# A four-layer graph network on one core: buffers, order and engines of the normalisation in the first and last node phase

## What is computed

```python
# layer 0: skip = per-irrep linear of x, weighted by the node's attribute; an angle from the summed messages
#          gives cos and sin, and  out = cos(angle) * skip + sin(angle) * summed
x = layernorm(x + layer_0(x, ...))          # over the 160 features, eps 1e-5
# layer 3:
fs   = silu(out_s[:, :64])
gate = sigmoid(out_s[:, 64:96])
gv   = gate[:, :, None] * out_v             # 32 vectors of 3
x = layernorm(x + concat(fs, gv))
```

## Time and profile before

| | |
|---|---|
| median of 3 runs | 6049.73 us (6048.89 to 6055.41) |
| the profiled execution | 6039.83 us, of which its span is 6038.1 us |
| TensorE busy (share of the span) | 5207.7 us (86%) |
| VectorE busy | 4336.6 us (72%) |
| ScalarE busy | 3091.9 us (51%) |
| GpSimd busy | 3854.7 us (64%) |
| DMA | 139 GB/s over the span |

### The profile page before, as it was taken

The page is one execution under the profiler, slowest core; times in us unless marked ns, Lnnn a source line. Parts: engine busy times, 40 slices in busy tenths (PEclk is TensorE's granted clock), DMA queues, the critical chain, the costliest instruction groups (busy, mean ns, idle before and its releaser), DMA issues. The chain is left out here.

```text
span 6038.1 us, 126869 instructions
## 1 busy us (share of the span) xinstructions
PE 5207.7 (86%) x29532; PEld 4038.8 (67%) x29580; DVE 4336.6 (72%) x15122; ACT 3091.9 (51%) x6650; POOL 3854.7 (64%) x4249
## 2 busy tenths in 40 slices
PE   8898977659999799699978888679999989997776
PEld 6565656655666699577756566568888867776766
DVE  3577759874444488688867777568888877775988
ACT  5333327763444366444444443257777744443766
POOL 8687866656888688776614554556666668885222
PEclk9899989998999899899987777789999999998999
DMA  8577766655666676354533333223333335554665
GB/s 321 137 127 119 123 119 224 221 173 112 133 132 126 174 230 227 119 161 157 162 115 83 88 88 89 70 93 108 114 108 108 114 80 86 87 88 90 228 225 184
DMA packets 547954, 837.00 MB, mean 139 GB/s; under 512 B 200220, under 2 KB 298612, under 8 KB 544436
## 3 DMA queue, kind: packets, MB, share of 16 engines
q1 hardware_dynamic: 397235, 666.91, 35.1%
q0 software_dynamic: 150528, 167.91, 16.5%
HBM read 464.00 MB, written 369.33 MB: 138 GB/s over the span
## 5 line engine op out<-in xcount | busy, mean ns | idle before, releaser
L1162 POOL DMA_INDIRECT xg<-x,gidx x588 | 611.0, 1039 | 243.1 <-issue 169.9
L339 POOL DMA_INDIRECT agg<-summed,cidx x392 | 632.2, 1613 | 201.9 <-issue 113.1
L422 DVE TENSOR_TENSOR pr<-pf,ws 128x512 f32<-128x512 f32 x196 | 135.5, 691 | 463.3 <-PE pf L509 356.4
L1337 ACT ACTIVATE ob<-po 128x416 f32<-128x416 f32 (+1 forms) x392 | 197.7, 504 | 353.9 <-PE po L1414 176.9
L1173 POOL DMA_INDIRECT agg<-summed,cidx x196 | 316.4, 1615 | 77.7 <-issue 57.6
L1822 POOL DMA_INDIRECT old_a<-agg,cidx_a x196 | 188.8, 963 | 262.9 <-DMA agg<-new_a,cidx_a 109.4
L1828 POOL DMA_INDIRECT agg<-new_a,cidx_a x196 | 194.8, 994 | 238.5 <-DVE new_a L1924 183.8
L538 PEld LDWEIGHTS pc<-ob,same 128*128 128x128 f32 x1960 | 276.1, 192 | 81.1 <-issue 81.1
L2112 PE MATMUL pk_n<-wsb,xta_n 128*128 128x192 f32 x784 | 222.7, 368 | 112.0 <-ACT xtb_n L2127 112.0
L2205 POOL TENSOR_TENSOR rs_n<-ve_n,wsb 128x4 f32<-128x4 f32 x98 | 98.8, 1008 | 336.8 <-DVE nm_n L2193 336.8
L1400 PE MATMUL ph<-esT,wsb 128*128 128x512 f32 x588 | 303.0, 597 | 2.4 <-DMA trow<-in_src_r 2.4
(11 more groups left out here) (366 smaller groups left out, 17869.3 us busy)
## 6 DMA issues: line engine op xcount, KB each, us to landing
ar_n<-agg SPq DMA_DIRECT2D x194, 322.0 KB
agg<-zero SPq DMA_DIRECT2D x50, 768.0 KB
ar_n<-agg SPq DMA_DIRECT2D x97, 384.0 KB
agg<-zero SPq DMA_DIRECT2D x50, 704.0 KB
ar_n<-agg SPq DMA_DIRECT2D x97, 352.0 KB
agg<-zero_h SPq DMA_DIRECT2D x25, 1288.0 KB, 5.4
agg<-zero SPq DMA_DIRECT2D x50, 644.0 KB
x<-xn_n SPq DMA_DIRECT2D x97, 324.0 KB, 2.5
```

What stands on the lines that cost most here:

```text
L339: pool.indirect_dma_start(agg, bass.IndirectOffsetOnAxis(ap=cidx[r][:, t:t + 1], axis=0), summed[u][:, t, :], None, compute_op=ALU.add).th ...
L1162: pool.indirect_dma_start(xg[s][r][:, t, 0:XR], None, x, bass.IndirectOffsetOnAxis(ap=gidx[s][r][:, t:t + 1], axis=0)).then_inc(gathered[r ...
L1337: a.activation(ob[u][:, t, :], po[:, t % 2, 0:TW], ACT.Copy).then_inc(ob_ok, 1)
```

## The change

In both phases `y`, `mv`, `rs` and `nr` get four buffers (index r % 4), and the waits that guard them reach back to chunk c - 4 instead of c - 2. VectorE's variance step is gone: GpSimd makes `ve` and `nm` at the start of its deviation, behind a new wait for the join. ScalarE normalises one turn later (lag 5 for 4, and 4 for 3). In node phase 0 GpSimd's factors run one turn later (lag 2 for 1), and the sines wait for ScalarE's own cosine of the turn before. In node phase 3 ScalarE makes `ga` = `gt` + 1 in an instruction of its own, from a constant column `one`, and VectorE's gate is one product over all four t. Node phase 1 starts with eight `fence` steps on VectorE.

```diff
@@ node_phase_01
-        y = each(2, sb, "y", [P, T, D])
+        y = each(4, sb, "y", [P, T, D])
-        mv = sb("mv", [P, T, 2])
+        mv = each(4, sb, "mv", [P, T, 2])
-        rs = each(2, sb, "rs", [P, T])
-        nr = each(2, sb, "nr", [P, T])
+        rs = each(4, sb, "rs", [P, T])
+        nr = each(4, sb, "nr", [P, T])
@@ scalar
                 a.wait_ge(cf_ok, due(NCF * (c - 1)))
+                a.wait_ge(sc_ok, 2 * c)
...
-            node_pipeline(a, ((0, copy_turned), (4, normalise)) + (((1, sines),) if l == 0 else ()))
+            node_pipeline(a, ((0, copy_turned), (5, normalise)) + (((1, sines),) if l == 0 else ()))
@@ vector
-                v.wait_ge(xn_ok, due(T * (c - 1)))
+                v.wait_ge(xn_ok, due(T * (c - 3)))
...
             def join(c, r, k, parts):
-                v.wait_ge(ve_ok, 2 * c)
+                v.wait_ge(rs_ok, due(2 * (c - 3)))
                 v.wait_ge(st_ok, 8 * c + 4)
                 fence(v)
                 for t in range(T):
-                    v.bn_aggr(mv[:, t, :], st[:, t, :]).then_inc(st_ok, 1)
-
-            def variance(c, r, k, parts):
-                u = r % 2
-                v.wait_ge(st_ok, 8 * c + 8)
-                v.wait_ge(rs_ok, due(2 * (c - 1)))
-                v.tensor_scalar(ve[u][:], mv[:, :, 1], EPS, None, ALU.add).then_inc(ve_ok, 1)
-                v.tensor_scalar(nm[u][:], mv[:, :, 0], -1.0, None, ALU.mult).then_inc(ve_ok, 1)
-
-            node_pipeline(v, ((3, skips), (3, sums), (3, moments), (3, join), (3, variance)))
+                    v.bn_aggr(mv[r % 4][:, t, :], st[:, t, :]).then_inc(st_ok, 1)
+
+            node_pipeline(v, ((3, skips), (3, sums), (3, moments), (3, join)))
@@ gpsimd
             def deviation(c, r, k, parts):
                 u = r % 2
-                pool.wait_ge(xn_ok, due(T * (c - 1)))
-                fence(pool)
+                pool.wait_ge(xn_ok, due(T * (c - 3)))
+                fence(pool)
+                pool.wait_ge(st_ok, 8 * c + 8)
+                fence(pool)
+                pool.tensor_scalar(ve[u][:], mv[r % 4][:, :, 1], EPS, None, ALU.add).then_inc(ve_ok, 1)
+                pool.tensor_scalar(nm[u][:], mv[r % 4][:, :, 0], -1.0, None, ALU.mult).then_inc(ve_ok, 1)
                 pool.wait_ge(ve_ok, 2 * c + 2)
                 fence(pool)
-                pool.tensor_tensor(rs[u][:], ve[u][:], wt("mhalf"), ALU.pow).then_inc(rs_ok, 1)
+                pool.tensor_tensor(rs[r % 4][:], ve[u][:], wt("mhalf"), ALU.pow).then_inc(rs_ok, 1)
...
-            node_pipeline(pool, ((1, factors), (3, deviation), (1, attribute)) + (((0, angles),) if l == 0 else ()))
+            node_pipeline(pool, ((2, factors), (3, deviation), (1, attribute)) + (((0, angles),) if l == 0 else ()))
@@ node_phase_1, vector
+            for _ in range(LEAD):
+                fence(v)
@@ node_phase_3 (buffers, join and deviation as above)
+        ga = each(2, sb, "ga", [P, T, V1])
+        one = sb("one", [P, 1])
@@ scalar
                 a.activation(sg[u][:, :, 0:S0], ss[u][:, :, 0:S0], ACT.Silu).then_inc(act_ok, 1)
+                a.wait_ge(act_ok, 3 * c + 1)
+                a.activation(ga[u][:], gt[u][:], ACT.Identity, bias=one[:, 0:1], scale=1.0).then_inc(act_ok, 1)
...
-            node_pipeline(a, ((0, copy_turned), (3, normalise), (1, gates)))
+            a.wait_ge(folded, 3)
+            node_pipeline(a, ((0, copy_turned), (4, normalise), (1, gates)))
@@ vector
+            v.memset(one[:], 1.0).then_inc(folded, 1)
...
-                for t in range(T):
-                    last = v.scalar_tensor_tensor(sg[u][:, t, S0:D].rearrange("p (u c) -> p u c", c=3), gt[u][:, t, :].unsqueeze(2).to_broadcast([P, V1, 3]), 1.0,
-                                                  sv[u][:, t, :].rearrange("p (u c) -> p u c", c=3), ALU.add, ALU.mult)
-                last.then_inc(sg_ok, 1)
+                v.tensor_tensor(sg[u][:, :, S0:D].rearrange("p t (u c) -> p t u c", c=3), sv[u][:].rearrange("p t (u c) -> p t u c", c=3),
+                                ga[u][:].unsqueeze(3).to_broadcast([P, T, V1, 3]), ALU.mult).then_inc(sg_ok, 1)
```

More of the change, by code:

```diff
@@ L44 @@
 VW = 168
+LEAD = 8
 EPS = 1e-5
@@ L675, in normalise @@
                 for t in range(T):
-                    a.activation(xn[r][:, t, 0:D], y[u][:, t, :], ACT.Identity, bias=nr[u][:, t:t + 1], scale=rs[u][:, t:t + 1]).then_inc(xn_ok, 1)
+                    a.activation(xn[r][:, t, 0:D], y[r % 4][:, t, :], ACT.Identity, bias=nr[r % 4][:, t:t + 1], scale=rs[r % 4][:, t:t + 1]).then_inc(xn_ok, 1)
             if l == 0:
                 a.wait_ge(folded, 4)
-            node_pipeline(a, ((0, copy_turned), (4, normalise)) + (((1, sines),) if l == 0 else ()))
+            node_pipeline(a, ((0, copy_turned), (5, normalise)) + (((1, sines),) if l == 0 else ()))
         @block.vector
@@ L2114, in skip @@
                 last.then_inc(k_ps, 1)
-            pe.wait_ge(folded, 2)
+            pe.wait_ge(folded, 3)
             node_pipeline(pe, ((0, turn_rows), (1, skip)))
@@ L2141, in normalise @@
                 for t in range(T):
-                    a.activation(xn[r][:, t, :], y[u][:, t, :], ACT.Identity, bias=nr[u][:, t:t + 1], scale=rs[u][:, t:t + 1]).then_inc(xn_ok, 1)
-            node_pipeline(a, ((0, copy_turned), (3, normalise), (1, gates)))
+                    a.activation(xn[r][:, t, :], y[r % 4][:, t, :], ACT.Identity, bias=nr[r % 4][:, t:t + 1], scale=rs[r % 4][:, t:t + 1]).then_inc(xn_ok, 1)
+            a.wait_ge(folded, 3)
+            node_pipeline(a, ((0, copy_turned), (4, normalise), (1, gates)))
         @block.vector
         def _(v):
+            v.memset(one[:], 1.0).then_inc(folded, 1)
             v.tensor_scalar(wt("na_3")[:, 96:192], wt("na_3")[:, 96:192], 0.5, None, ALU.mult).then_inc(folded, 1)
```

36 lines of the change are left out of this document (18 added, 18 removed).

## The result

The changed kernel takes 6013.6 us in the median of five runs (6001.69 to 6021.03), the kernel before 6048.89 in the five runs that stand for it now (6041.1 to 6055.41): 0.9945 of it, with a 95% interval of 0.9933 to 0.9956. That is faster by 33 us by the ratio and by 35 us by the medians, inside the stated range, but 22 us above the forecast of 5992. The profiled execution's span is 6011.6 us, against 6038.1.

What follows compares the result with a forecast made beforehand. Phase 0 was taken as bound by a GpSimd-ScalarE ring, phase 3 by VectorE. Savings of 45.6 us (phase 3) and 12.6 (phase 0) sum to 58 off the 6049.7 median, giving 5992; range 5966 to 6022.

Steps and rivals of the forecast that it cites:

- a ring of GpSimd and ScalarE: Node phase 0 before: GpSimd's at, rs, nr, then ScalarE's normalising and sines, back to at; 4.39 us a turn.
- VectorE's own turn: Node phase 3 before: VectorE itself sets the pace, 4.60 us a turn with no idle time named in the rows.
- the second rival: Phase 0 gains nothing or loses (0 to +16 us), GpSimd's path being too long; phase 3 as forecast; 6004 to 6020; chance 0.24.
- (a) the gate: Node phase 3, VectorE: four gate instructions become one 128x384 product, gate to total 0.89 to 0.68 us, saving 0.21 a turn.
- The fourth rival: Phase 3's one product runs at the dear row's 840 ns: -17 us there, phase 0 -30, so 6020; chance 0.11.
- (b) the join: Node phase 3: constant and negation leave VectorE, join to next layer 0.67 to 0.41 us, saving 0.26 (0.17 to 0.34).
- ScalarE's and the DMA's room: Node phase 3: ScalarE's work grows to 3.5 us, under 4.14; DMA rises from 224 to 249 GB/s, with room for loads.
- ScalarE's wait for nr: Node phase 3: 140.8 us before; its being gone was named as a sign that the forecast is right.
- 0.17 + 0.43 = 0.6 us: Node phase 0, GpSimd: cost a turn of adding ve and nm ahead of the power, giving a turn of 4.1 to 4.25.
- The second path: Node phase 0: a ring over two turns between VectorE and GpSimd, 8.4 us for two turns, 4.2 each.
- The fifth: Slower through instruction fetching at the jumps of shifted loops; 6062 at the deciding point, 6002 if partial; chance 0.06.
- The small edits: Cosine wait, four buffers, memset and third TensorE count cost no time; eight steps ahead of node phase 1 at most 0.4 us.

## Why the prediction was right in one phase and wrong in the other

- **What bounds the kernel.** Node phase 0 as a ring of GpSimd and ScalarE: shown, by the operations put into it alone (0.90 us a turn more while VectorE had less to do). Node phase 3 as VectorE's own turn: its two savings came out in full, and one of them by itself. The total is inside the range partly by luck: node phase 3 gained 6.8 us more than forecast, node phase 0 lost 11.0 instead of gaining 12.6, and the range reached up far enough to hold the second rival.
- **Phase 3, (a) the gate.** 0.21 us a turn forecast; 0.89 to 0.68 in the rows, 0.22 in the run with the gate alone. The row with the same repeated input (549 ns) was the right one to take: the gate takes 551. The fourth rival fell with it.
- **Phase 3, (b) the join.** 0.26 forecast between 0.17 and 0.34; 0.67 - 0.35 = 0.32 measured, near the upper end, which fits VectorE's next waits being handled under the joins. Together 0.53 instead of 0.47 us a turn, 52.4 instead of 45.6 us. ScalarE's and the DMA's room was as worked out: 43.7 busy us of 50, and 252 GB/s where 249 were expected. ScalarE's wait for nr, which was to be gone, fell from 140.8 to 29.4 us.
- **Phase 0, the mechanism.** That the ring's waits go and GpSimd's own row is late next was right, and so was that VectorE would idle behind cf (57.4 us). But GpSimd's turn, forecast at 4.2 to 4.35, came out over 4.44, which the prediction had named as a sign of being wrong.
- **Phase 0, the size.** The term that failed is "0.17 + 0.43 = 0.6 us" for the two operations. In the trace after it is 0.34 + 0.31 + 0.41 less the 0.19 that stood there: 0.87 us, and 0.90 in the old ring. That is the turn shown; over the loop's turns from 960 to 1290 us the mean is 0.31 + 0.31 + 0.41 less 0.22, 0.81 us. I had taken 0.17, the mean of the starts from at to cf and from cf to the power, for both new starts; the dependent power was sized rightly (0.41 for 0.43). The rest of the row came out near the upper end: 4.56 - 0.87 = 3.69 us a turn with the jump in it, against 3.5 to 3.65 and 0.07 for the jump; by the loop's passes it is 36.8 / 8 - 0.81 = 3.79, a little above. With 0.87 and the upper end the same sum is 3.65 + 0.87 = 4.52, and with the jump's 0.07 it is 4.59: slower than 4.44. The saving of 12.6 us became a loss of 11.0.
- **The second path,** the ring over two turns at 4.2: not seen as a limit. With the operations on VectorE the hand-over ran at 34.2 / 8 = 4.27 us a turn including the jump, with no named wait of weight on VectorE; with them on GpSimd, GpSimd waits for VectorE's join for 1.4 us in the whole phase, so its own row is longer than that path.
- **The rivals.** What happened is the second one, by its time too (6004 to 6020 forecast, 6013.6 measured), but by the starts of the two operations and not by operations held up beside VectorE: nr's median went from 303 to 237 ns and the copy's from 189 to 347, which together make 0.05 us a turn from nr to the next th. VectorE's sums took 373 to 382 ns each, as before, though the power ran beside them. The fifth, instruction fetching, did not happen in the change, but it is real: 52 us in one loop, where I had thought 1 us a pass to be its likely size and the runs show 6.
- **The small edits.** The eight steps are worth nothing here, as forecast. The sum over the stages is -52.4 + 11.0 + 2.6 for node phase 1 and 12 for the stages ahead, whose lengths vary that much from run to run: -27, against -26.5 between the two spans.

## What to carry to other kernels

An operation of four numbers is not priced by its 0.2 us but by its place in an in-order row: here the way to the first, an immediate and a dependent successor made two of them 0.8 to 0.9 us. So before work is moved off the engine that is busiest on average, lay out the receiving engine's turn start by start, with waits of the same kind taken from the same queue, and try the engine that waits most; here that was ScalarE, with the deviation a turn later. And when a loop's body is as long as the 283 instructions here, look at the "issue" waits and the instruction packets of the loops behind an edit, not only at the edited stage.

## What the runs showed of the hardware that was not expected

- The place of a loop's code: 60 instructions of shift turned passes of 34.8 us into 41, and 16 in another kernel turned them back, with 37 instruction blocks of 8 KB moved in 300 us instead of 2, in a stage whose text is the same.
- GpSimd's power of 128x4 takes longer beside VectorE's long products. In node phase 3 before, when it started beside the layer's first product, and after, when its start fell on the gate's (5701.08 and 5701.07 in one turn; lines L2205 and L2211):

```profile
L2205 POOL TENSOR_TENSOR rs_n<-ve_n,wsb x98: 1007/1008/1042, 5583.7 to 6031.5; 128x4 f32<-128x4 f32 x98
```

```profile
L2211 POOL TENSOR_TENSOR rs_n<-ve_n,wsb x98: 1036/1438/1443, 5610.5 to 6005.0; 128x4 f32<-128x4 f32 x98
```

0.43 us more, while the gate keeps its 0.55. ScalarE waits 29.4 us in the phase for the nr behind it, VectorE, which sets the pace, not at all. That it is held until the gate has read its two inputs fits these rows; no run was made to separate it.
